# Two chained recurrences on one core: loop bodies of 64 steps on three engines, and a state sum in two column halves

## The reference

```
z = sigmoid(xz + rz)      r = sigmoid(xr + rr)
hh = relu(xh + r * rh)    h_new = z * h + (1 - z) * hh
```

```
r = sigmoid(xr + rr)      c = relu(xc + r * rc)
h_new = (1 - a) * h + a * c
```

## Time and profile before

| | us |
|---|---|
| median of 3 runs | 4424.12 (4422.9 to 4429.71) |
| profiled execution | 4430.53 |
| its span | 4428.7 |
| GRU loop on VectorE | from 16.23 to about 2317 |
| softmax stage | up to 2352.69 |
| AGRU loop | from there to the end |

### The profile page before, as it was taken

The page is one execution under the profiler, slowest core; times in us unless marked ns, Lnnn a source line. Parts: engine busy times, 40 slices in busy tenths (PEclk is TensorE's granted clock), DMA queues, the critical chain, the costliest instruction groups (busy, mean ns, idle before and its releaser), DMA issues.

```text
span 4428.7 us, 336421 instructions
## 1 busy us (share of the span) xinstructions
PE 4372.4 (99%) x131196; PEld 3968.0 (90%) x131196; DVE 4196.2 (95%) x24625; ACT 2286.8 (52%) x9363; POOL 2717.1 (61%) x6154
## 2 busy tenths in 40 slices
PE   8999999999999999999998999999999999999999
PEld 7888888888888888888887999999999999999998
DVE  8999999999999999999998999999999999999999
ACT  5666666666666666666654444444444444444444
POOL 6777777777777777777773444444444444444444
PEclk9999999999999999999998999999999999999999
DMA  3333333333333333334334555555555555554554
GB/s 110 115 116 123 115 116 123 115 115 121 117 115 120 119 115 120 119 115 121 118 123 129 129 132 128 128 132 128 128 133 128 128 133 128 128 133 129 127 133 115
DMA packets 169275, 544.13 MB, mean 123 GB/s; under 512 B 31644, under 2 KB 38060, under 8 KB 169260
## 3 DMA queue, kind: packets, MB, share of 16 engines
q1 hardware_dynamic: 169260, 543.93, 44.3%
HBM read 405.24 MB, written 138.56 MB: 123 GB/s over the span
## 4 chain that ended last, share of the span: by engine, by line
DVE 52%; PE 21%; issue 20%; DMA 3%; DVEq 2%; SPq 1%; ACT 0%; ACTq 0%; PEldq 0%
DVE vec_bank L525 12%; DVE gated L448 8%; DVE state L538 7%; DVE a_new L532 6%; DVE vec_bank L455 5%; DVE gated L519 5%; DVE vec_bank L464 5%; DVE h L475 4%; PE r_bank_a L561 4%; PE r_bank_b L561 3%; DMA logits<-logit_rows 2%; PE logit_bank L623 2%; PE z_bank_b L569 2%; PE z_bank_a L569 2%; PE c_bank_a L561 1%
## 5 line engine op out<-in xcount | busy, mean ns | idle before, releaser
L331 POOL TENSOR_TENSOR a_kept<-attn_rest,state 128x128 f32<-128x128 f32 x2048 | 933.6, 456 | 1173.6 <-DVE state L538 1139.0
L314 POOL TENSOR_TENSOR kept<-z_gate,h 128x128 f32<-128x128 f32 x2048 | 933.6, 456 | 533.8 <-ACT z_gate L360 512.0
L304 POOL TENSOR_TENSOR prod<-h,qw 128x128 f32<-128x128 f32 x2050 | 934.6, 456 | 0.0
L569 PE MATMUL r_bank_a<-x,weights 64*64 64x128 f32 x8200 | 881.7, 290 | 12.8 <-ACT r_gate L389 7.1
L569 PE MATMUL r_bank_b<-x,weights 64*64 64x128 f32 x8192 | 892.8, 295 | 0.0
L569 PE MATMUL z_bank_a<-x,weights 64*64 64x128 f32 x8200 | 853.9, 283 | 0.0
L569 PE MATMUL z_bank_b<-x,weights 64*64 64x128 f32 x8192 | 843.3, 283 | 0.0
L623 PE MATMUL logit_bank<-prod,row_sum 64*64 64x128 f32 x8208 | 798.5, 270 | 8.6 <-ACT logit_rows L349 5.0
L464 DVE SCALAR_TENSOR_TENSOR vec_bank<-vec_bank,z_rest 128x64 f32<-128x64 f32 x4096 | 735.9, 225 | 0.4 <-issue 0.3
L475 DVE TENSOR_TENSOR h<-vec_bank,kept 128x64 f32<-128x64 f32 x4096 | 721.3, 218 | 0.0
L389 ACT ACTIVATE r_gate<-r_bank_a 128x128 f32<-128x128 f32 x1024 | 284.0, 277 | 837.5 <-PE r_bank_a L561 837.5
(11 more groups left out here) (119 smaller groups left out, 17857.4 us busy)
## 6 DMA issues: line engine op xcount, KB each, us to landing
x<-in_keys_t SPq DMA_DIRECT2D x512, 256.0 KB, 3.7
gru_outputs<-h SPq DMA_DIRECT2D x256, 512.0 KB, 2.9
x<-gru_outputs SPq DMA_DIRECT2D x512, 256.0 KB, 3.7
attn<-attention SPq DMA_DIRECT2D x512, 256.0 KB, 3.9
logits<-logit_rows SPq DMA_DIRECT2D x258, 8.0 KB
time_rows<-logits SPq DMA_DIRECT2D x2, 896.0 KB, 7.0
attention<-time_rows SPq DMA_DIRECT2D x2, 896.0 KB, 5.5
weights<-in_weight_columns SPq DMA_DIRECT2D x2, 176.0 KB, 3.7
```

The lines of the kernel that those rows point to most:

```text
L304: nc.gpsimd.tensor_tensor(prod[:, (s - 1) % BODY, gcols(g)], h_at(s - 1)[:, gcols(g)], qw[:, gcols(g)], ALU.mult).then_inc(prod_ready[g], 1)
L314: nc.gpsimd.tensor_tensor(kept[:, g], z_gate[:, g], h_at(s - 1)[:, gcols(g)], ALU.mult).then_inc(kept_ready[g], 1)
L331: nc.gpsimd.tensor_tensor(a_kept[:, s % 2, gcols(g)], attn_rest[:, s % 2, gcols(g)], state[:, (s - 1) % 2, gcols(g)], ALU.mult).then_inc(a ...
L569: last = nc.tensor.matmul(dst[lanes(half)], weights[lanes(1 - half), w], moving[lanes(1 - half)], start=start, stop=False, skip_group_chec ...
```

## The change

- VectorE, ScalarE and GpSimd write out 64 steps (`SPAN = 8 * BODY`) in a loop body instead of 8, in both loops. Their loops run 16 times instead of 128 times. TensorE and SyncE keep bodies of 8 steps.
- `r_ready` and `ar_ready` become two semaphores for each group, for even and for odd steps. The value VectorE and TensorE wait for is `s % 8 // 2 + 1` (`by_parity`). TensorE counts them down by 4 (`HALF`) instead of 8, at other matmuls. The extra wait for `r_summed` or `ar_summed` and the semaphore `bodies_begun` at the start of VectorE's body are gone.
- VectorE computes `due` in two registers taken in turn (`count`), for the next step, ahead of the b group's `gru_new` or `agru_new`.
- `agru_sum` becomes two instructions of 64 columns. Part 0 stands where the sum stood, part 1 behind `agru_cand`. Only part 1 signals `s_ready`.

```diff
+SPAN = 8 * BODY
...
-            with dve.Fori(0, T, BODY) as t0:
-                stored = t0 * ONES + 16
-                for s in range(BODY):
-                    due = t0 + (s + 2)
+            with dve.Fori(0, T, SPAN) as t0:
+                soon = count(0, t0, 2)
+                for s in range(SPAN):
+                    due = soon
+                    if s % CHUNK == 0:
+                        stored = t0 * ONES + 16 * (s // BODY + 1)
                     for g in GROUPS:
                         gru_gated(due, s, g)
                         gru_cand(due, s, g)
+                        if g == 1:
+                            soon = count(s + 1, t0, s + 3)
                         gru_new(due, s, g)
                         gru_h(due, stored, s, g)
...
             def gru_gated(due, s, g):
-                if s == 0:
-
-                    dve.wait_ge(r_summed[g], due)
-                    dve.sem_inc(bodies_begun, 1)
                 dve.wait_ge(rh_summed[g], due)
-                dve.wait_ge(r_ready[g], s + 2)
+                dve.wait_ge(r_ready[g][s % 2], by_parity(s))
...
-            def agru_sum(done, s, g):
-                dve.wait_ge(akept_ready[g], done)
-                dve.wait_ge(anew_ready[g][s % 2], ANEW[s % BODY])
-                nc.vector.tensor_tensor(state[:, s % 2, gcols(g)], a_new[:, s % 2, gcols(g)],
-                                        a_kept[:, s % 2, gcols(g)], ALU.add).then_inc(s_ready[g], 1)
+            def agru_sum(done, s, g, part):
+                c = PARTS[part][1]
+                if part == 0:
+                    dve.wait_ge(akept_ready[g], done)
+                    dve.wait_ge(anew_ready[g][s % 2], ANEW[s % BODY])
+                last = nc.vector.tensor_tensor(state[:, s % 2, gcols(g)][:, c], a_new[:, s % 2, gcols(g)][:, c],
+                                               a_kept[:, s % 2, gcols(g)][:, c], ALU.add)
+                if part == 1:
+                    last.then_inc(s_ready[g], 1)
...
                     agru_gated(due, s, 0)
-                    agru_sum(done, s - 1, 1)
+                    agru_sum(done, s - 1, 1, 0)
                     agru_cand(due, s, 0)
+                    agru_sum(done, s - 1, 1, 1)
                     agru_new(due, pairs, s, 0)
                     agru_gated(due, s, 1)
-                    agru_sum(due, s, 0)
+                    agru_sum(due, s, 0, 0)
                     agru_cand(due, s, 1)
+                    agru_sum(due, s, 0, 1)
+                    soon = count(s + 1, t0, s + 3)
                     agru_new(due, pairs, s, 1)
...
-                        pe.wait_ge(r_ready[o], seen_by_pe(s, o))
+                        pe.wait_ge(r_ready[o][(n - 1) % 2], by_parity(n - 1))
```

More of the change, by code:

```diff
@@ L56, in part_sems, with parity_sems @@
             return [[sem(f"{name}_{'ab'[g]}{part}") for part, _ in PARTS] for g in GROUPS]
+        def parity_sems(name):
+            return [[sem(f"{name}_{'ab'[g]}_{('even', 'odd')[parity]}") for parity in range(2)] for g in GROUPS]
         weights = sb("weights", [P, 11, U])
@@ L322, in _ @@
                 product(BODY, g)
-            with pool.Fori(0, T, BODY) as t0:
-                for s in range(BODY):
+            with pool.Fori(0, T, SPAN) as t0:
+                for s in range(SPAN):
                     done, due = t0 + (s + 1), t0 + (s + 2)
@@ L349, in copy_logits @@
                 nc.scalar.activation(logit_rows[:], logit_bank[:, 0:COLS], ACT.Copy).then_inc(logits_copied, BODY)
[L351 to L354, removed]
+            with act.Fori(0, T, SPAN) as t0:
+                for s in range(SPAN):
+                    if s % BODY == 2:
+                        copy_logits(t0 + (s - 2))
                     due = t0 + (s + 2)
@@ L383, in _ @@
             rest(0)
-            with act.Fori(0, T, BODY) as t0:
-                for s in range(BODY):
+            with act.Fori(0, T, SPAN) as t0:
+                for s in range(SPAN):
                     done, due = t0 + (s + 1), t0 + (s + 2)
@@ L473, in gru_h, with count @@
                         if g == 0 and s % CHUNK == 0:
-                            dve.wait_ge(outs_stored[s // CHUNK], stored)
+                            dve.wait_ge(outs_stored[s // CHUNK % 2], stored)
                     last = nc.vector.tensor_tensor(h_at(s)[:, gcols(g)][:, c], new[:, c], kept[:, g, c], ALU.add)
                 last.then_inc(h_ready[g], 1)
-            with dve.Fori(0, T, BODY) as t0:
-                stored = t0 * ONES + 16
-                for s in range(BODY):
-                    due = t0 + (s + 2)
+            counts = [dve.alloc_register(f"dve_count_{i}") for i in range(2)]
+            def count(i, base, more):
+                dve.reg_add(counts[i % 2], base, more)
+                return counts[i % 2]
+            with dve.Fori(0, T, SPAN) as t0:
+                soon = count(0, t0, 2)
+                for s in range(SPAN):
+                    due = soon
+                    if s % CHUNK == 0:
+                        stored = t0 * ONES + 16 * (s // BODY + 1)
                     for g in GROUPS:
@@ L546, in _ @@
+            with dve.Fori(0, T, SPAN) as t0:
+                done, soon = t0 + 1, count(0, t0, 2)
+                for s in range(SPAN):
+                    due = soon
+                    if s % CHUNK == 0:
+                        pairs = t0 * PAIRS + 32 * (s // BODY + 1)
                     agru_gated(due, s, 0)
-                    agru_sum(done, s - 1, 1)
+                    agru_sum(done, s - 1, 1, 0)
                     agru_cand(due, s, 0)
+                    agru_sum(done, s - 1, 1, 1)
@@ L549, in _ @@
                     agru_new(due, pairs, s, 0)
                     agru_gated(due, s, 1)
-                    agru_sum(due, s, 0)
+                    agru_sum(due, s, 0, 0)
                     agru_cand(due, s, 1)
+                    agru_sum(due, s, 0, 1)
+                    soon = count(s + 1, t0, s + 3)
                     agru_new(due, pairs, s, 1)
                     done = due
-            agru_sum(T + 1, T - 1, 1)
+            for part in range(2):
+                agru_sum(T + 1, T - 1, 1, part)
```

72 lines of the change are left out of this document (34 added, 38 removed).

## The result

| | before | after |
|---|---|---|
| median, us | 4426.3 (4422.9 to 4429.71, 4 runs) | 4599.65 (4598.3 to 4602.81, 4 runs) |
| profiled execution, us | 4430.53 | 4602.81 |
| its span, us | 4428.7 | 4601.0 |
| pieces of code in queue 14 | 6 | 572 |

The changed kernel takes 1.0393 times as long [1.0375, 1.0411]. It is slower by 173 us. I had predicted 4324, a gain of 107 (97 + 118 - 108).

What follows compares the result with a forecast made beforehand. VectorE was taken to bound the GRU loop, a ring through four engines the AGRU loop, TensorE close behind. 4430.5 - 97 (GRU) - 118 (AGRU) + 108 (code fetched at 30 ends) = 4323.5 us; range 4222 to 4412.

Steps and rivals of the forecast that it cites:

- Sum in two halves: AGRU loop: half the sum between gated and cand brings cand 0.33 us behind gated, gaining 0.07 a step.
- 0.133 at 64: AGRU loop, VectorE: operations of 64 columns issue 0.133 us apart, against 0.20 at 128 columns.
- Register addition: Moved off the wait for group a's gate: up to 0.09 us in a's AGRU ring, 0.03 a GRU step.
- AGRU step of 1.88: AGRU loop: a step falls from 1.96 to 1.88 us, range 1.86 to 1.94; 8 steps take 15.27.
- the ring: AGRU loop: the repeating chain of operations through four engines, 1.96 us a step before, 1.80 after the change.
- TensorE's floor: AGRU loop: TensorE works 0.93 us a group without a stop, so a step can't be under 1.86.
- Fewer ends: Both loops: fewer body ends, 0.48 us saved at seven of eight GRU ends; loop totals 97 and 118 us.
- The 0.48: GRU loop: gated a starts 0.48 us late at a body's end, put down to VectorE's own branch back.
- Remaining ends: Both loops: 30 branches back fetch code again at 3.6 us each, 108 us; case given 0.65.
- the clock: Rival, body ends: TensorE's clock falls, an end costs 7.1 to 8.9 us; ends that dear (4400 up) got 0.13.
- a mean below 0.98 over the loops: Both loops: PEclk, TensorE's granted clock, below 0.98 would show the prediction wrong on the clock.
- In between nothing waits: Inside the 64-step bodies: no engine stops for code between the ends; the sum has no term for it.

Runs made afterwards that it cites:

- e10: The changed kernel with 8-step bodies, the logits stored half a body earlier and the whole sum behind cand: 4288.09 us, 0.9683 of before.
- e5: The changed kernel with 8-step bodies and the sum in one piece ahead of cand: 4335.16 us, 0.9800 of before.
- e3: The changed kernel, still with 64-step bodies, with the sum in one piece ahead of cand: 4544.34 us, 1.0268 of before.
- e6: The changed kernel with 8-step bodies, halves kept, and GpSimd's AGRU a_kept on 16 of 128 columns (another result): 4267.1 us, one run.
- e4: The changed kernel, still with 64-step bodies, with SyncE's logits store issued half a body earlier: 4515.44 us, 1.0199 of before.
- e12: The kernel before with only the register addition moved ahead of new b, in both loops, 8-step bodies: 4357.07 us, 0.9834 of before.

## Why the prediction was wrong

- **Sum in two halves: wrong.** I gave it 0.07 a step ("costs nothing while that gap is there"). It costs 0.11 in most steps: 55 us at 64 steps, 86 at 8. I followed `a_kept` to TensorE, where it is late by nothing that the rows show, and didn't lay GpSimd's operation beside VectorE's. My own numbers held it: `a_kept` would run from cand b + 0.58 (0.20 + 0.38) to + 1.03, and the next part 0 would start at + 0.80 (0.93 for a group, less 0.33, plus 0.20), within that. The failed step is the "0.133 at 64" for part 0, which holds only while GpSimd is idle: cand a comes 0.49 behind gated a and cand b 0.42 behind gated b, instead of 0.33. With that VectorE, which I had at 0.87 for a group and no bound, needs 1.03 and 0.95. The Trainium skill, SBUF — State Buffer, section SBUF: two separate sides, says that VectorE and GpSimd share one pair of ports by an exclusive lock for a whole instruction, and that a VectorE operation takes part in it where it reads two SBUF operands. The traces agree: part 0 (both operands in SBUF) ends 0.08 behind GpSimd, while operations with one operand in a PSUM bank take as long beside GpSimd as without it, gated in the changed kernel (0.28), cand in e10 (0.30) and new in e5 (0.29). By that rule and these times the forecast would have had no gain from this edit.
- **Register addition: half right.** In AGRU right and by the right amount (0.31 behind the sigmoid, 72 us alone). In GRU the 0.03 a step isn't there: 2.155 with the addition at either place, where the sum has 2.13. 26 us of it fall away.
- **AGRU step of 1.88:** the 8 steps for which I had 15.27 take 15.90, 0.63 x 128 = 81 us. Without the halves they take 15.33 (e3), but that the forecast comes so near to this is luck. I had the ring at 1.80 and TensorE's floor above it; the runs show no such floor (1.80 in e6), and a ring of 1.87 because the whole sum stands between gated and cand (e5).
- **Fewer ends: wrong in GRU.** The 0.48 that went was the cover of the logits' store. What took its place costs 84 us (e4), more than the 112 x 0.48 = 54 that went: the store lands some 0.8 us too late for the copy (2.97 against 2.155 in that step), and the 0.48 had hidden most of that (before, this step was 0.08 over). I asked what hides under which work for the sum and not for the time that I removed. The 0.06 that I had read behind the end of a body I then left out without a reason: the usual 8 steps take 17.38 without the logits' wait (e4), 0.14 over 8 x 2.155 and not 0.09, 7 us.
- **Remaining ends: right mechanism, mis-sized.** Code is fetched at each, in hundreds of pieces, and the stop of 3.9 to 4.0 us is near the 3.6. What I had as a rival, the clock, is part of every end: 0.50 for some 3 us behind each. About 5.07 instead of 3.6 makes 44 us. I had held the stop too short for the clock to fall, because the one stretch at 0.59 came behind a longer one. My sign for it, a mean below 0.98 over the loops, was too coarse: some 3.4 us at the lower level in 150 leave the mean at 0.985.
- **"In between nothing waits": wrong.** VectorE also stops for code inside the bodies, as here, an operation in the middle of a step:

```profile
1217.89 0.36 DVE L468 SCALAR_TENSOR_TENSOR vec_bank<-vec_bank,z_rest 128x64 f32<-128x64 f32 x2 [0.30 <-issue]
```

The waits of VectorE in the changed kernel show four lines of that kind beside those of gated:

```profile
DVE vec_bank L468 <- issue: 11.3, 32, 0.7
...
DVE h L479 <- issue: 6.1, 32, 0.2
...
DVE state L551 <- issue: 4.2, 16, 0.3
DVE vec_bank L535 <- issue: 3.7, 16, 0.2
```

Together 25 us, and some 7 more ahead of gated in AGRU (67.5 less 15 ends of 4.0). The Trainium skill, Runtime: NRT & Kernel Launch, section Instruction fetch mechanics, calls the crossing from one block of code to the next mostly hidden, which is less than the "nothing waits" that I made of it. Here it was not quite hidden: 0.19 to 0.35 us a time by these lines (6.1 / 32 and 11.3 / 32).

Added up, 81 + 26 + 84 + 7 + 44 + 32 = 274, against the 276 between 4324 and 4600. Some of these overlap, above all at an end, where the logits' wait has cover again, so that the last few us of the agreement are luck. The dear ends alone would not have turned the gain into a loss: 4215.5 + 30 x 5.07 = 4368, still below 4426. The held half and the uncovered store did.

## What to carry to other kernels

A stall that goes may have been the cover of a slower transfer: before a periodic stop is removed, list every DMA whose landing is waited for in the stretch behind it. When an instruction of VectorE with both operands in SBUF is moved, lay it beside GpSimd's timeline, not only beside the engines that wait for its result. A longer loop body pays only while the code of each engine is still there at the branch back; look at the pieces in the code queue, and if there are hundreds, go back to the short body before trying a hint.

## What the runs showed of the hardware that I had not expected

- VectorE's loop body of 139 rows (GRU, 8 steps) and 150 rows (AGRU, 16 steps) is kept at the branch back; 275 rows (GRU, 16 steps) is fetched at every one. In instructions of the trace that is 189 and 247 kept, 372 fetched. The limit lies between; where a body stands in the program was not varied.
- A branch back to code that is gone stops the engine for 3.9 to 4.0 us, whether the body is 275 or 1098 rows long. The clock then stays at its lower level for about 3 us, so that an end costs 5.
- Loading ahead of the branch takes off 4.2 of these 5 us.
- A VectorE addition of 128 x 64 from two SBUF operands ends 0.08 us behind a GpSimd operation that was running when it started, and takes up to 0.37 instead of 0.21.
- A register addition that carries a semaphore's wait costs the instruction behind it 0.09 us (0.40 against 0.31 behind the sigmoid, e12). One without a wait, in the GRU, cost nothing that the steps show (2.156 and 2.154).
